# Edge features turned in groups of two pairs, thirteen one-hot buffers and a single rank bank in the target stage of a graph network

## What is computed

```python
h = relu(layernorm(x)); x = x + attention(h, src, dst, W, ...)        # layer 0, 4 heads of 32
h = relu(layernorm(x))
msg = concat([h[src], h[dst], edge_attr])                              # 128 + 128 + 64
out = segment_sum(relu(msg @ W1 + b1) @ W2 + b2, src)
return x + out
```

## Time and profile before

| | us |
|---|---|
| median of three runs | 5811.69 |
| the three runs | 5804.10, 5811.69, 5815.06 |
| the profiled execution, its time | 5807.29 |
| the profiled execution, its span | 5805.4 |

### The profile page before, as it was taken

How to read it: one execution, slowest core, us unless ns; L and a number is a source line. 1 busy time by engine, 2 the same in 40 slices (tenths; PEclk the granted TensorE clock), 3 DMA queues, 4 the chain that set the end, 5 groups by cost and what they waited for, 6 DMA issues and landing times.

```text
span 5805.4 us, 160391 instructions
## 1 busy us (share of the span) xinstructions
PE 5114.6 (88%) x34498; PEld 4012.9 (69%) x34499; DVE 4028.8 (69%) x14406; ACT 2891.4 (50%) x8241; POOL 3923.5 (68%) x3713
## 2 busy tenths in 40 slices
PE   4888888888888886899999999999987999999999
PEld 3677777776677775667666666666665777777777
DVE  6777777777777778555555555555555888888887
ACT  3555555555555553333333333333224777777776
POOL 4777777777777775677777777777776545555553
PEclk6898888888888887999999999999998999999999
DMA  4422222222222225899888899988896999999997
GB/s 108 161 54 52 52 53 53 52 53 53 53 52 52 53 62 165 261 262 269 261 263 260 255 262 260 257 261 253 256 256 182 214 214 211 213 216 215 213 214 187
DMA packets 860289, 993.31 MB, mean 171 GB/s; under 512 B 307992, under 2 KB 663224, under 8 KB 859774
## 3 DMA queue, kind: packets, MB, share of 16 engines
q1 hardware_dynamic: 662494, 608.23, 40.1%
q0 software_dynamic: 190592, 378.22, 24.3%
q10 hardware_dynamic: 6816, 3.38, 0.2%
HBM read 726.65 MB, written 262.76 MB: 170 GB/s over the span
## 4 chain that ended last, share of the span: by engine, by line
PE 55%; DMA 12%; DVE 10%; issue 10%; POOL 7%; DVEq 4%; ACT 2%; POOLq 0%; SPq 0%; ACTq 0%
PE bank L1525 12%; PE bank L1684 11%; PE bank L1617 7%; DMA xr<-arena 7%; PE bank L1619 7%; POOL xr L542 7%; PE bank L1674 6%; DMA arena<-p_tab,arena 3%; PE bank L1453 3%; DVE arena L1042 2%; DVEq L246 2%; DVE arena L935 2%; PE bank L1607 1%; DMA arena<-h_tab,arena 1%; PE bank L1665 1%
## 5 line engine op out<-in xcount | busy, mean ns | idle before, releaser
L494 POOL DMA_INDIRECT arena<-h_tab,arena x1612 | 1591.7, 987 | 582.9 <-issue 399.5
L542 POOL DMA_INDIRECT xr<-arena x1612 | 1587.3, 985 | 510.7 <-issue 350.3
L1525 PE MATMUL bank<-arena 128*128 128x136 f32 x6448 | 1299.7, 329 | 96.6 <-DVE arena L1042 8.1
L703 ACT ACTIVATE arena<-bank 128x256 f32<-128x256 f32 x1612 | 595.9, 385 | 1405.6 <-PE bank L1619 1050.2
L556 POOL DMA_INDIRECT arena<-p_tab,arena x428 | 668.4, 1562 | 658.7 <-DMA arena<-p_tab,arena 443.4
L1525 PEld LDWEIGHTS bank<-arena 128*128 128x128 f32 x6448 | 966.3, 211 | 201.8 <-issue 109.0
L621 ACT ACTIVATE arena<-bank 128x256 bf16<-128x256 bf16 x1612 | 618.2, 384 | 888.9 <-PE bank L1453 833.6
L1617 PE MATMUL bank<-arena 128*128 128x256 f32 x3224 | 1010.3, 395 | 42.4 <-DVE arena L1236 25.2
L1619 PE MATMUL bank<-arena 128*128 128x256 f32 x3224 | 972.5, 383 | 28.6 <-DVE arena L1252 25.5
L1684 PE MATMUL bank<-arena 128*128 128x257 f32 x3424 | 898.8, 385 | 3.8 <-ACT arena L780 3.2
L1042 DVE TENSOR_TENSOR arena<-arena,bank 128x272 f32 x1612 | 692.2, 429 | 181.5 <-PE bank L1525 163.7
(11 more groups left out here) (253 smaller groups left out, 6596.8 us busy)
## 6 DMA issues: line engine op xcount, KB each, us to landing
arena<-xr SPq DMA_DIRECT2D x428, 516.0 KB, 3.9
arena<-q_tab SPq DMA_DIRECT2D x1612, 128.0 KB
arena<-in_edge_attr SPq DMA_DIRECT2D x61, 832.0 KB
arena<-rel_tab SPq DMA_DIRECT2D x124, 224.0 KB
arena<-h_tab,arena POOLq DMA_INDIRECT x1612
xr<-arena POOLq DMA_INDIRECT x1612
arena<-rel_tab SPq DMA_DIRECT2D x124, 192.0 KB
xr<-arena SPq DMA_DIRECT2D x26, 516.0 KB
```

The lines of the kernel that those rows point to most:

```text
L494: pool.indirect_dma_start(G[:, q, t, :], None, h_tab, bass.IndirectOffsetOnAxis(ap=idx[:, q, t:t + 1], axis=0)).then_inc(sem(f"gath{q}"), 16)
L542: pool.indirect_dma_start(xr, bass.IndirectOffsetOnAxis(ap=pos[:, q, t:t + 1], axis=0), Rb[:, t, :], None).then_inc(sem(f"scat{m}"), 16)
L1525: last = pe.matmul(PSB[3 + t % 2][:, k * H * MW:(k + 1) * H * MW], OH[:, (t + 2 * q) % 4, k * P:(k + 1) * P], flat(msg[:, t, :, :]), start ...
```

## The change

Edge features are turned by groups of two pairs (EG = 2, four tiles), so that the 13 pairs of a batch make seven groups (NEG), the last one with a single pair. A group goes into bank 4 or bank 6 in turn, and one copy takes it out. Group j + 1 is turned at t = 4j, ahead of main(t), group 0 of the next batch at t = 22 of this one, copied out at t = 24. There are 13 one-hot buffers (RO), and DVE makes five ahead (HOTS). Bank 6 being taken, all three rank products use bank 5, each after DVE has used the one before; they move to t = 11, 15, 18 on PE and 13/14, 17/18, 20/21 on DVE. Counts are four tiles in each of iterations 1 to 7. In the node phase the second rank product moves behind `node(0)`, with the third, and DVE handles all three after node 0. For space, `EAT` and `t49` lie over tables (`lastE`, `dBE`) that only the attention stage reads. ACT's steps move by one or two tiles. POOL's program is unchanged.

```diff
+RO = 13
+HOTS = 5
+EG = 2
+NEG = -(-(BT // 2) // EG)
...
-        EAb, EAT = S([2, BT, DE]), S([2, P])
-        OHT, oh49 = S([4, P]), S([2, BT, NT], BF16)
-        cnt26, t49, posf, padf = S([NT], BF16, BT), S([BT, NT]), S([BT]), S([BT])
+        EAb, OHT, oh49 = S([2, BT, DE]), S([RO, P]), S([2, BT, NT], BF16)
+        cnt26, posf, padf = S([NT], BF16, BT), S([BT]), S([BT])
+        t49 = dBE[:, 0:BT * NT].rearrange("p (t b) -> p t b", b=NT)
+        EAT = lastE.bitcast(F32)[:, 0:2 * EG * P].rearrange("p (g k e) -> p g k e", k=EG, e=P)
...
@@ SP, load_windows
-                            sp.wait_ge(sem("eaT_ps"), b * (BT // 2))
+                            sp.wait_ge(sem("eaT_ps"), b * NEG)
@@ ACT, targets
-                    if ahead and t == 9:
+                    if ahead and t == 8:
                         counts_out(b + 1)
-                    if part is not None and t == 22:
+                    if part is not None and t == 24:
                         act.wait_ge(sem("pq_ps"), NCH * NQ + part + 1)
@@ DVE, targets
-                    if not (first and t < 4):
-                        dve.wait_ge(sem("main_done"), B + t - 3)
-                    V.tensor_scalar(OHT[:, (t + 2 * q) % 4, :], DB[:, t * P:(t + 1) * P], pcol, None,
+                    if not (first and t < RO):
+                        dve.wait_ge(sem("main_done"), B + t - RO + 1)
+                    V.tensor_scalar(OHT[:, t % RO, :], DB[:, t * P:(t + 1) * P], pcol, None,
...
-                def ea_out(j):
-                    Gp = b * (BT // 2) + j
-                    dve.wait_ge(sem("eaT_ps"), Gp + 1)
-                    if not (first and j < 2):
-                        dve.wait_ge(sem("main_done"), 2 * Gp - 2)
-                    V.tensor_copy(EAT[:, (j + q) % 2, :], PSB[4][:, 0:P]).then_inc(sem("ea_out"), 1)
-                hot(0)
-                hot(1)
+                def ea_out(c, p, j):
+                    u, n = p * NEG + j, len(egroup(j))
+                    dve.wait_ge(sem("eaT_ps"), c * NEG + j + 1)
...
+                    V.tensor_copy(EAT[:, u % 2, 0:n, :], PSB[(4, 6)[u % 2]][:, 0:n * P].rearrange("p (k e) -> p k e", e=P)).then_inc(sem("ea_out"), 1)
+                for t in range(HOTS):
+                    hot(t)
+                if first:
+                    ea_out(b, q, 0)
                 for t in range(BT):
-                    if t % 2 == 0:
-                        ea_out(t // 2)
-                    if t < BT - 2:
-                        hot(t + 2)
+                    if t % (2 * EG) == 2 and t // (2 * EG) + 1 < NEG:
+                        ea_out(b, q, t // (2 * EG) + 1)
+                    if t < BT - HOTS:
+                        hot(t + HOTS)
...
-                        if t in (11, 14, 18):
-                            rank(r, {11: 0, 14: 1, 18: 2}[t])
-                        if t in (12, 15, 19):
-                            own(r, s, {12: 0, 15: 1, 19: 2}[t])
+                        if t in (13, 17, 20):
+                            rank(r, {13: 0, 17: 1, 20: 2}[t])
+                        if t in (14, 18, 21):
+                            own(r, s, {14: 0, 18: 1, 21: 2}[t])
...
+                        if t == 24:
+                            ea_out(r, s, 0)
@@ DVE, node phase
                 if c == 0:
-                    for m in range(2):
+                    for m in range(3):
                         rank(0, m)
                         own(0, 0, m)
                 if c == 1:
-                    rank(0, 2)
-                    own(0, 0, 2)
                     total(0)
@@ PE, rank
-                if m == 2:
-                    pe.wait_ge(sem("rk_used"), 3 * r + 1)
-                elif m == 0:
+                if m == 0:
                     pe.wait_ge(sem("c26_ready"), r + 1)
...
+                if not (isinstance(r, int) and r == 0 and m == 0):
+                    pe.wait_ge(sem("rk_used"), 3 * r + m)
+                o = PSB[5]
@@ PE, targets
+                def turn_ea(c, p, j):
+                    u = p * NEG + j
+                    if not (first and c is b and j < 2):
+                        pe.wait_ge(sem("ea_out"), c * NEG + j - 1)
+                    for k in egroup(j):
+                        done = pe.transpose(PSB[(4, 6)[u % 2]][:, (k - j * EG) * P:(k - j * EG + 1) * P], flat(EAb[:, p, 2 * k:2 * k + 2, :]), ident)
+                    done.then_inc(sem("eaT_ps"), 1)
...
-                    if t % 2 == 1 and t < BT - 1:
-                        turn_ea((t + 1) // 2)
+                    if t % (2 * EG) == 0 and t // (2 * EG) + 1 < NEG:
+                        turn_ea(b, q, t // (2 * EG) + 1)
                     main(t)
...
-                        if t < 9:
-                            counts(r, s, 3 * t, 3 * t + 3)
-                        if t in (10, 13, 17):
-                            rank(r, s, {10: 0, 13: 1, 17: 2}[t])
-                        if t == 18:
+                        if 1 <= t < 8:
+                            counts(r, s, 4 * t - 4, 4 * t)
+                        if t in (11, 15, 18):
+                            rank(r, s, {11: 0, 15: 1, 18: 2}[t])
+                        if t == 20:
                             total(r)
-                        if t == 21 and part is not None:
+                        if t == 22:
+                            ea_there(r, s, last)
+                            turn_ea(r, s, 0)
+                        if t == 23 and part is not None:
                             source_part(part, r)
@@ PE, node phase
             rank(0, 0, 0)
-            rank(0, 0, 1)
             for c in range(NCH):
                 node(c)
                 if c == 0:
+                    rank(0, 0, 1)
                     rank(0, 0, 2)
```

45 lines of the change are left out of this document (22 added, 23 removed).

## The result

| | before | after |
|---|---|---|
| median, us | 5810.42 (4 runs, 5804.10 to 5815.06) | 5865.7 (4 runs, 5863.7 to 5869.69) |
| after / before | | 1.0097, 95% interval 1.0079 to 1.0114 |
| span of the profiled execution | 5805.4 | 5861.6 |

The change makes the kernel 1% slower: 55 us, where 1.8 were forecast. In the kernel after, the scatter is L548, the copy into `Rb` L709, the two products L1631 and L1634, the one-hot L1242, `ea_out` L1258, the block one-hots L1197, `rank` and `own` L1208 and L1214, tags L1249 and L1250, and x1 of the node phase L1179.

The account below looks back on a forecast made before the run. The prediction took the stage from 2350 to 4433 us to be a POOL queue of scatters, 1.276 us each. Terms 0 + 0 + 0 + 1.3 + 0.5 + 0 = +1.8 us on the 5811.7 median gave 5813.5, range 5801 to 5828.5.

Parts of the forecast that it names:

- R3: Rival, scatter stage: PE is the bound after all, so edge stalls and one-hot waits go; -93 us, 5720; 4%.
- (a): Edge features turned two pairs at a time, a group ahead: 0.95 us less DVE a batch, beside POOL; 0 us.
- (b): Thirteen one-hot buffers, five ahead: PE's batch-edge stall can go, 1.1 us a batch, but POOL stays late; 0 us.
- (c): One bank for the loop's three rank products: waits for DVE covered by PE's lead; 0 us while it stands.
- R1: Rival, scatter stage: waits on the single rank bank make PE's side the bound; +130 us, 5943; 5%.
- R4: Rival, scatter stage: POOL's long scatters get shorter, DVE doing less beside them; at most 22 us, 5791; 5%.
- (d): Node phase, single rank bank: node 1 starts 6.5 us late, some comes back; +1.3 us, bounds 0 to +4.4.
- (e): First tile: DVE's tags, and so the first scatter, come later; +0.5 us, bounds -0.3 to +1.5.
- The mark of a first scatter beyond 2360: Start of the scatter stage: sign that the node-phase forecast (d) is wrong; about 2356.8 was expected.
- (f): Scatter stage: POOL's 22 us over its minimum stay, L1191 and L1208 keeping their number; 0 us, bounds -11 to +11.
- R2: Rival, batch edges: bursts of five one-hots hold up POOL, 1.5 us a batch; 95 us, 5908; 4%.

Follow-up runs that it names:

- e3: Changed kernel with the next batch's five one-hots made one in each of iterations 21 to 25, not in a burst; 5829.58 us, ratio 1.0024.
- e6: Kernel before with five more one-hots into an unread spare buffer at t = 5, away from the block one-hots; 5822.6 us, ratio 1.0010.
- e4: Kernel before with the four block one-hots made a second time into an unread spare buffer; 5833.91 us, ratio 1.0029.
- e9: Changed kernel with the block one-hots put ahead of the five one-hots at the batch edge; 5868.48 us, ratio 1.0096.
- e14: Changed kernel with DVE also waiting for the matmuls of the batch's second tile ahead of the block one-hots; ratio 1.0085.
- e13: Changed kernel with DVE also waiting for the matmuls of the batch's first tile ahead of the block one-hots; 5820.45 us, ratio 1.0025.
- e1: Changed kernel with two one-hots made ahead of a batch in place of five; 5861.76 us, ratio 1.0081.
- e5: Kernel before with five more one-hots into an unread spare buffer at t = 0, ahead of the block one-hots; 5892.35 us, ratio 1.0134.
- e7: Changed kernel with a 49-column copy out of PSUM between the five one-hots and the block one-hots; 5877.38 us, ratio 1.0108.

## Why the prediction was wrong

**What bounds the kernel** was right: POOL without a wait, a 1.276 us period, a lead of over 20 us. So were the consequences drawn from it: parts (a), (b) and (c) cost POOL no wait, and PE's gain at the edge disappears into the lead. The rival R3 is refuted by that, and the single rank bank showed no price in the stage (R1 by that place): e3, which keeps it, has POOL's waits at 2.9 us in all above 0.305 each. R4 went the other way: the scatters got longer. The stall at the counts was expected to go and only shrank, from 1.50 to 0.91 us, which cost POOL nothing.

**Parts (d) and (e)** were right in mechanism and too small: +3.3 and +0.8 us measured, +1.3 and +0.5 worked out, inside their bounds of 4.4 and 1.5. Node 1 was 6.7 us late (6.5 worked out); of the 5.2 us that were to come back, 3.4 did. The mark of a first scatter beyond 2360 was passed (2362.1), 3.1 us of it by an attention stage that ended later.

**The step that failed is (f).** POOL's 22 us over its minimum were put down to L1191 and L1208, which "keep their number", so 0 with bounds of 11 either way. Measured: 76.3 us above 971 ns per scatter where 22.1 were, +54.2. The lengthening belongs not to an instruction but to what stands directly ahead of it on DVE. The row was there: the earlier trace rows has a scatter of 1.21 us beside L1191, and the timeline of that edge has DVE arriving at it from a wait; the change takes precisely that wait away (the L1252 at t = 0 with its wait for PE). (e) names it, for the first batch, as a wait that "drops out"; what it did for POOL at the other edges was never asked. The bound of 11 was half of a number, not a bound from a row; the row to take was the longest scatter, 2.49 us, at an edge without that wait: 1.5 us more at each of 62 edges is 93 us, and an upper end that took it in would have held the 54.

**Rival R2** came nearest, and its mark (mean above 995 ns) is what showed it. But it was priced by the burst's own 1.5 us, which e6 shows to be free, and the argument against it, "mean less median over all scatters is 14 ns, though 1612 one-hots run beside them", is about one-hots beside a scatter and says nothing of one-hots ahead of L1191. 54 us over 62 batches, 0.9 us each, was the measured price, not 1.5. The rule of the Trainium skill that whoever gets the shared ports holds them for the whole instruction ("SBUF — State Buffer", section "Who interferes with whom") was set aside on the same argument. With it the kernel before agrees: all but two of its scatters beside L1191 go on when the instruction that they meet is through, at 1.30, 1.73 or 2.10 us. The kernel after doesn't: 37 of 49 are held beyond it, to the end of all four. That one-hots by themselves don't shut POOL out is shown by e6. The same section of the Trainium skill infers, and says that it is inferred, that descriptor generation is not stalled by a tensor_tensor; e4, in which nothing but a second set of these is added and the scatters get 18 us longer in all, speaks against that, and the measurement decides.

**R1** didn't occur in the change, but e9 and e14 each ran into it, at 54 and 49 us. The margin of 0.047 us a tile was real; its 1.2 us a batch is used up by 1.68 us of block one-hots ahead of PE's first one-hot (e9) or by 1.4 us more of stall at the counts (e14).

## What to carry to other kernels

When an engine that never waits is the bound, look at the longest forms of its instruction and what stands directly ahead of them on the engine beside which they got long; each is a price that an innocent reorder can multiply. A wait on an engine off the critical path may be doing work for the one that is on it: before removing one, ask who uses the pause. And when a repair trades the one limit for the other at equal time, as e9 did, busy and idle time of the bounding instruction tell them apart where the total can't.

## What the runs showed of the hardware

A scatter of 128 rows by indirect DMA takes POOL 0.971 us in the median plus 0.305 of issue, with 1612 one-hots of DVE beside 1612 scatters; five in a row, 310 more in all, left the mean at 986 ns (e6). Four tensor_tensor instructions in a row, of which one starts every 0.37 to 0.43 us, do lengthen the first scatter that starts beside them: where it takes over 1.0 us, it ends 0.93 us behind a change of DVE from one instruction to the next, so at 1.30, 1.73, 2.10 or 2.53 us behind the start of the first, and at no other time (before, after, e13). With a wait and two short instructions ahead of the four, or a standstill of 0.45 us, that is the next change, and the scatter takes at most 1.33 and 1.24 us, but for two in the kernel before; directly behind six one-hots 37 of 49 wait for the last change (after), and the longest scatters are 2.4 to 2.7 us (after, e1, e5, e7). In e4, where eight block one-hots follow each other, one was held for 4.02 us. Beside POOL's arithmetic, a tensor_tensor of 128x896 fp32 took DVE 2.58 us instead of 1.08; moved away from it, it took 1.08.
